# Layer norm statistics in two steps, the start of the reciprocal root on GpSimd, and one group of products with values

## What is computed

```python
def _layernorm(x, axis=-1, eps=1e-05):
    m = jnp.mean(x, axis=axis, keepdims=True)
    v = jnp.var(x, axis=axis, keepdims=True)
    return (x - m) / jnp.sqrt(v + eps)

def step(carry, blk):                      # one chunk of 128 tokens
    S, z = carry
    q_c, k_c, v_c = blk
    scores = jnp.einsum('bhcd,bhkd->bhck', q_c, k_c)
    scores = jnp.where(mask, scores, 0.0)
    num = jnp.einsum('bhck,bhke->bhce', scores, v_c) + jnp.einsum('bhcd,bhde->bhce', q_c, S)
    den = scores.sum(-1) + jnp.einsum('bhcd,bhd->bhc', q_c, z)
    S = S + jnp.einsum('bhkd,bhke->bhde', k_c, v_c)
    z = z + k_c.sum(axis=2)
    return ((S, z), (num, den))

xn = _layernorm(x, axis=-1)
x = x + attention(xn, w_attn, w_proj) + ffn(xn, gate_w, gate_b, expert_bias, w1, b1, w2, b2)
```

## Time and profile before

| what | value |
|---|---|
| median of 3 runs | 570.75 us (570.57 to 571.49) |
| the profiled execution | 570.87 us, its span 569.1 us |
| PE busy, whole span | 491.9 us, 86% |
| DVE busy | 430.7 us, 76% |
| ACT busy | 277.7 us, 49% |
| POOL busy | 283.8 us, 50% |
| first `scores` of the pipeline's steady part to its last | 38.11 to 289.65 us |

### The profile page before, as it was taken

How to read it: one execution, slowest core, us unless ns; L and a number is a source line. 1 busy time by engine, 2 the same in 40 slices (tenths; PEclk the granted TensorE clock), 3 DMA queues, 4 the chain that set the end, 5 groups by cost and what they waited for, 6 DMA issues and landing times.

```text
span 569.1 us, 17397 instructions
## 1 busy us (share of the span) xinstructions
PE 491.9 (86%) x6065; PEld 394.9 (69%) x6065; DVE 430.7 (76%) x917; ACT 277.7 (49%) x535; POOL 283.8 (50%) x448
## 2 busy tenths in 40 slices
PE   3599999899998999889985169989989989999992
PEld 1477877777877778677863068868868868877871
DVE  3779898998989899898776927766757666766671
ACT  0447767767777777667755023333333333333330
POOL 2645658666677576685553232343433443342421
PEclk9589999999999999999998569999999999999997
DMA  8322654645645546545323221212221222221000
GB/s 283 109 74 75 197 178 146 187 140 171 200 145 168 152 159 202 163 147 183 112 77 112 92 75 48 76 56 80 66 65 49 66 65 67 65 65 41 31 6 0
DMA packets 34016, 62.44 MB, mean 110 GB/s; under 512 B 5517, under 2 KB 9998, under 8 KB 33808
## 3 DMA queue, kind: packets, MB, share of 16 engines
q1 hardware_dynamic: 28944, 48.74, 27.5%
q0 software_dynamic: 4992, 12.60, 7.4%
HBM read 50.57 MB, written 13.50 MB: 113 GB/s over the span
## 4 chain that ended last, share of the span: by engine, by line
PE 73%; DVE 18%; issue 4%; DMA 1%; ACT 1%; POOL 1%; DVEq 0%; POOLq 0%; ACTq 0%
PE ps L551 19%; PE ps L565 18%; PE ps L380 6%; PE ps L342 5%; PE ps L407 4%; PE ps L391 3%; PE ps L448 3%; PE ps L421 3%; PE ps L434 3%; DVE rsn L604 2%; DVE AR L669 2%; PE ps L356 2%; PE ps L529 2%; DVE rsn L602 2%; PE ps L363 1%
## 5 line engine op out<-in xcount | busy, mean ns | idle before, releaser
L551 PEld LDWEIGHTS ps<-AR,W 128*128 x1872 | 131.6, 99 | 39.9 <-issue 1.0
L565 PE MATMUL ps<-W,ST 128*128 x624 | 150.8, 326 | 7.0 <-issue 7.0
L551 PE MATMUL ps<-AR,W 128*128 128x128 f16 x1872 | 155.8, 221 | 0.8 <-ACT AR L1038 0.8
L1097 POOL TENSOR_TENSOR W<-ST,W 128x512 f16<-128x512 f32 x64 | 74.4, 1162 | 79.9 <-ACT W L1001 79.7
L1137 POOL DMA_INDIRECT out<-AR x39 | 39.6, 1016 | 127.4 <-DVE AR L922 127.4
L890 DVE SCALAR_TENSOR_TENSOR ST<-ps,TAs,B1S 128x512 f32<-128x512 f32 x78 | 58.5, 749 | 58.7 <-PE ps L551 58.0
L1047 ACT ACTIVATE ST<-ST 128x512 f16<-128x512 f32 x78 | 49.2, 630 | 97.1 <-DVE ST L890 93.7
L669 DVE TENSOR_TENSOR AR<-ps,CT 128x512 f32<-128x512 f32 x128 | 82.0, 683 | 11.9 <-PE ps L380 11.9
L902 DVE SCALAR_TENSOR_TENSOR ST<-ST 128x512 f16<-128x512 f32 x78 | 53.6, 688 | 15.6 <-ACT ST L1047 15.2
L1132 POOL DMA_INDIRECT AR<-scr,AR x39 | 48.0, 1230 | 28.6 <-issue 11.0
L1088 POOL TENSOR_SCALAR AR<-AR,CT 128x256 f32<-128x256 f32 x64 | 59.3, 938 | 4.0 <-DVE AR L663 4.0
(11 more groups left out here) (145 smaller groups left out, 772.6 us busy)
## 6 DMA issues: line engine op xcount, KB each, us to landing
ST<-in_w SPq DMA_DIRECT2D x128, 256.0 KB, 4.2
scr<-XR SPq DMA_DIRECT2D x32, 256.0 KB, 2.1
XR<-in_x SPq DMA_DIRECT2D x32, 128.0 KB, 4.6
AR<-in_b SPq DMA_DIRECT2D x1, 1024.0 KB, 4.9
AR<-in_wall SPq DMA_DIRECT2D x1, 776.0 KB, 4.7
AR<-scr,AR POOLq DMA_INDIRECT x39, 3.6
out<-AR POOLq DMA_INDIRECT x39
AR<-in_wp SPq DMA_DIRECT2D x1, 256.0 KB, 5.1
```

The lines of the kernel that those rows point to most:

```text
L551: a = e.matmul(dst, W[:, off:off + 57472][:, bass.ds(at[s], 128)], XT16[s % 2][:, xl * 256 + k * 128:xl * 256 + (k + 1) * 128], start=(n = ...
L565: a = e.matmul(PS[4 + s % 2][:, 0:w], src[h % 4][:, fs], W[:, off:off + 57344 + w][:, bass.ds(at[s], w)], start=(f == 0 and w == 512), sto ...
L1097: e.tensor_tensor(lo_, src, hi, ALU.subtract).then_inc(p_wlo, 1)
```

## The change

`na` is split. `sums(c)` is the first instruction; `na(c)` is now the second alone, and stands on DVE behind `res` instead of ahead of it. Adding eps and the first guess go to GpSimd, to the head of `nn`: one instruction adds eps, one multiplies the variance's bits (as an integer) by -0.5 and adds the constant, so that three instructions on DVE become two on GpSimd. `nn` waits for the semaphore of `na` of the pair's second chunk.

The two halves of `pv` become one, at the end of TensorE's period. `inter` takes the place of the first half, begins the accumulation in PS[5] and waits for `y1` of the chunk before; only in a sequence's first chunk does `pv` begin it. Masks 0 and 1 now wait for the whole `pv` of the chunk before, not for its first half. On GpSimd `km` stands ahead of the first `w_lo`.

```diff
@@ tensor
             def inter(c):
...
+                e.wait_ge(S["y1"], c)
                 for g in range(2):
                     for i in range(2):
                         j = 2 * g + i
                         a = e.matmul(PS[5][:, j * 128:(j + 1) * 128], T32[:, g, 4 * i:4 * i + 4, :],
-                                     QK[c % 2][:, g * 128:(g + 1) * 128], start=False, stop=True,
+                                     QK[c % 2][:, g * 128:(g + 1) * 128], start=(j == 0), stop=True,
...
-            def pv(c, i):
-                e.wait_ge(s_[2 * i], c + 1)
-                e.wait_ge(s_[2 * i + 1], c + 1)
-                if i == 0:
-                    e.wait_ge(S["vh"], c + 1)
-                    if c >= 1:
-                        e.wait_ge(S["y1"], c)
...
+            def pv(c):
+                e.wait_ge(S["vh"], c + 1)
+                if c >= 1:
+                    e.wait_ge(S["y1"], c)
+                for i in range(2):
+                    e.wait_ge(s_[2 * i], c + 1)
+                    e.wait_ge(s_[2 * i + 1], c + 1)
...
+                                             start=(c % CPB == 0 and j == 0), stop=True, skip_group_check=True)
+                a.then_inc(S["pv"], 1)
...
                 if on(p - 3):
-                    pv(p - 3, 0)
+                    inter(p - 3)
                 mxa(p)
-                if on(p - 3):
-                    inter(p - 3)
...
                 if on(p - 3):
-                    pv(p - 3, 1)
+                    pv(p - 3)
@@ vector
+            def sums(c):
+                e.wait_ge(d_x[c % R], 16 * (c // R + 1))
+                if c >= 1:
+                    e.wait_ge(S["na"], c)
+                e.bn_stats(st6[:, :], XR[c % R][:, 256:512]).then_inc(S["sums"], 1)
+
             def na(c):
...
-                e.tensor_scalar(r_[:, 1], mv[:, c % 4 - 1:c % 4 + 1, 1], 1e-5, None, ALU.add).then_inc(dv.up(), 1)
-                e.wait_ge(dv.sem, dv.n)
-                e.tensor_scalar(r_[:, 2].bitcast(I32), r_[:, 1].bitcast(I32), 1, None,
-                                ALU.logical_shift_right).then_inc(dv.up(), 1)
-                e.wait_ge(dv.sem, dv.n)
-                e.tensor_scalar(r_[:, 0].bitcast(I32), r_[:, 2].bitcast(I32), -1.0, float(0x5f3759df),
-                                ALU.mult, ALU.add).then_inc(S["na"], 1)
+                e.bn_aggr(mv[:, c % 4, :], st6[:, :]).then_inc(S["na"], 1)
...
             def s_mask(c, r):
                 e.wait_ge(S["sc"], c + 1)
                 if c >= 1:
-                    e.wait_ge(pv_[r // 2], c)
+                    e.wait_ge(S["pv"], c)
...
                 if on(p + 2):
-                    na(p + 2)
+                    sums(p + 2)
                 if on(p - 4):
                     res(p - 4)
+                if on(p + 2):
+                    na(p + 2)
@@ gpsimd
             def nn(c):
...
-                e.wait_ge(S["na"], c // 2 + 1)
+                e.wait_ge(S["na"], c + 1)
+                if c >= 4:
+                    e.wait_ge(S["nb"], c - 3)
+                e.tensor_scalar(r_[:, 1], mv[:, c % 4 - 1:c % 4 + 1, 1], 1e-5, None, ALU.add).then_inc(po.up(), 1)
+                e.wait_ge(po.sem, po.n)
+                e.tensor_scalar(r_[:, 0].bitcast(I32), r_[:, 1].bitcast(I32), -0.5, float(0x5f3759df),
+                                ALU.mult, ALU.add).then_inc(po.up(), 1)
+                e.wait_ge(po.sem, po.n)
...
-                w_lo(2 * (p - 5))
                 if on(p - 2):
                     km(p - 2)
+                w_lo(2 * (p - 5))
```

More of the change, by code:

```diff
@@ L81, in program @@
         mv = sb("mv", [128, 4, 2], F32)
-        rsn = sb("rsn", [128, 2, 4, 2], F32)
+        rsn = sb("rsn", [128, 2, 2, 2], F32)
         nv = sb("nv", [128, 4], F32)
@@ L238, in program @@
         v_sq, t_sq, v_sv, a_wa, v_wa, v_bm = (sem(n) for n in ("v_sq", "t_sq", "v_sv", "a_wa", "v_wa", "v_bm"))
-        names = ("na", "nn", "nb", "xh", "xl", "xt", "xTc", "qk", "relu", "exp", "phi", "km", "sc", "ktr", "kt",
+        names = ("sums", "na", "nn", "nb", "xh", "xl", "xt", "xTc", "qk", "relu", "exp", "phi", "km", "sc", "pv", "ktr", "kt",
                  "vg", "vh", "lg", "in", "st", "t32", "y1", "yt1", "y", "yt2", "y2", "pr", "res")
@@ L244, in program @@
         s_ = [sem(f"s_s{i}") for i in range(4)]
-        pv_ = [sem(f"s_pv{i}") for i in range(2)]
         v_wmx, a_wsc, a_whi, p_wlo = (sem(n) for n in ("v_wmx", "a_wsc", "a_whi", "p_wlo"))
@@ L391, in inter @@
                         a = e.matmul(PS[5][:, j * 128:(j + 1) * 128], T32[:, g, 4 * i:4 * i + 4, :],
-                                     QK[c % 2][:, g * 128:(g + 1) * 128], start=False, stop=True,
+                                     QK[c % 2][:, g * 128:(g + 1) * 128], start=(j == 0), stop=True,
                                      skip_group_check=True)
                 a.then_inc(S["in"], 1)
-            def pv(c, i):
-                e.wait_ge(s_[2 * i], c + 1)
-                e.wait_ge(s_[2 * i + 1], c + 1)
-                if i == 0:
-                    e.wait_ge(S["vh"], c + 1)
-                    if c >= 1:
-                        e.wait_ge(S["y1"], c)
[L403 to L411, removed]
+            def pv(c):
[5 more added lines that the diff above has]
+                    e.wait_ge(s_[2 * i + 1], c + 1)
+                    for g in range(2):
+                        for t in range(2):
+                            for o in range(2):
+                                j, b = 2 * g + i, 2 * t + o
+                                a = e.matmul(PS[5][32 * b:32 * b + 32, j * 128:(j + 1) * 128],
+                                             V32[c % 2][:, 8 * g + 4 * i + b, :],
+                                             S32[2 * i + t][:, (2 * g + o) * 128:(2 * g + o + 1) * 128],
+                                             start=(c % CPB == 0 and j == 0), stop=True, skip_group_check=True)
+                a.then_inc(S["pv"], 1)
             def st(c):
@@ L588, in vector @@
             e.tensor_tensor(SQ, WF, WF, ALU.mult).then_inc(v_sq, 1)
-            def na(c):
-                xb, m, r_ = XR[c % R], mv[:, c % 4, :], rsn[:, c // 2 % 2, :, :]
-                e.wait_ge(d_x[c % R], 16 * (c // R + 1))
-                e.bn_stats(st6[:, :], xb[:, 256:512]).then_inc(dv.up(), 1)
-                e.wait_ge(dv.sem, dv.n)
-                e.bn_aggr(m, st6[:, :]).then_inc(dv.up(), 1)
-                e.wait_ge(dv.sem, dv.n)
-                if c % 2 == 0:
-                    return
+            def sums(c):
[3 more added lines that the diff above has]
+                e.bn_stats(st6[:, :], XR[c % R][:, 256:512]).then_inc(S["sums"], 1)
+            def na(c):
+                e.wait_ge(S["sums"], c + 1)
                 if c >= 4:
                     e.wait_ge(S["nn"], c // 2 - 1)
-                e.tensor_scalar(r_[:, 1], mv[:, c % 4 - 1:c % 4 + 1, 1], 1e-5, None, ALU.add).then_inc(dv.up(), 1)
-                e.wait_ge(dv.sem, dv.n)
-                e.tensor_scalar(r_[:, 2].bitcast(I32), r_[:, 1].bitcast(I32), 1, None,
-                                ALU.logical_shift_right).then_inc(dv.up(), 1)
-                e.wait_ge(dv.sem, dv.n)
-                e.tensor_scalar(r_[:, 0].bitcast(I32), r_[:, 2].bitcast(I32), -1.0, float(0x5f3759df),
-                                ALU.mult, ALU.add).then_inc(S["na"], 1)
+                e.bn_aggr(mv[:, c % 4, :], st6[:, :]).then_inc(S["na"], 1)
             def nb(c):
@@ L616, in nb @@
                                 ALU.subtract, ALU.mult).then_inc(S["nb"], 1)
+            sums(0)
             na(0)
+            sums(1)
             na(1)
@@ L976, in vh @@
                 if c >= 2:
-                    e.wait_ge(pv_[1], c - 1)
+                    e.wait_ge(S["pv"], c - 1)
                 e.activation(V32[c % 2][:, :, 0:16], PS[1][:, 0:256].rearrange("p (h e) -> p h e", h=16), ACT.Copy,
@@ L984, in y1 @@
             def y1(c):
-                e.wait_ge(pv_[1], c + 1)
+                e.wait_ge(S["pv"], c + 1)
                 if c >= 1:
@@ L1117, in gpsimd @@
                 w_lo(2 * (p - 5) + 1)
-            e.wait_ge(pv_[1], NC)
+            e.wait_ge(S["pv"], NC)
             for i in range(NG):
```

## The result

| | median | runs | span of the profiled execution |
|---|---|---|---|
| before | 570.81 us | 4 (570.57 to 571.49) | 569.1 us (570.87 us in all) |
| changed | 551.58 us | 4 (549.11 to 552.69) | 549.7 us (551.49 us in all) |

The ratio is 0.9655, 95% interval 0.9622 to 0.9689: 19.2 us less. The forecast was 551.2 us, range 544.0 to 558.0.

What follows compares the result with a forecast made beforehand. PE was taken to bound one period and `scores` waiting for `res` the next. From 570.87 us, 16.1 us for that wait and 3.6 us for one group of `pv` were subtracted, giving 551.2 us, range 544.0 to 558.0.

Steps and rivals of the forecast that it cites:

- What bounds the kernel: First stage: PE sets the pace in one period; in the next, `scores` waiting for `res` costs 1.1 us.
- The wait goes (16.1 us): DVE work ahead of `res` leaves, so all 13 waits of `scores` for `res`, 16.1 us in all, vanish.
- The price of L602 and L604 is GpSimd's: On DVE, these 2-element instructions (0.69 and 1.08 us) are held up until GpSimd's running instruction ends, not busy.
- What comes to GpSimd: Two new `nn` instructions at 0.28 us each; `nn` lasts 3.9 us, leaving 1.3 us before `nb`; no cost booked.
- The one group of `pv` (3.6 us): On PE, `yt2` starts earlier but 16 more passes precede `scores`; net 0.10 us per regular period, 3.6 us in all.
- The rival with 554.8 us: The one group of `pv` on PE is worth nothing, only the wait for `res` goes; chance 0.16.
- The sum: Whole kernel: 570.87 - 16.1 - 3.6 = 551.2 us, nothing booked at the first stage's ends.
- The signs: First stage: `scores` waits for `res` under 2 us, PE over 98% busy, `yt2` waits nearly every period, `nb` never for `nn`.
- L596 (now L600): Rival: on DVE behind `res`, this instruction is stretched by 0.9 us each period, giving 566.6 us; chance 0.08.
- The slower rival: On GpSimd, `nn` becomes the bound; with every link held up it lasts 10.8 us, giving 617 us; chance 0.02.
- The whole drain: Rival: on PE, each of 29 periods saves 0.37 us of tiling switches, 10.7 us, giving 544.1 us; chance 0.07.

Runs made afterwards that it cites:

- e1_stats_only: Kernel before with only the statistics part of the change; `pv` in two halves and `km` as before: 551.5 us against 568.68 us, ratio 0.9689.
- e3_km_first: Kernel before with only `km` moved ahead of the first `w_lo` on GpSimd: 564.15 us against 568.68 us, ratio 0.9897.
- e11_small_w_lo: Kernel before with GpSimd's `w_lo` cut to 2 elements from the fifth tile on, second stage using high halves; only first stage read: odd periods 8.01 us.
- e8_long_nn: Changed kernel with twelve more links in `nn` on GpSimd: 572.02 us against 570.13 us for the kernel before, ratio 1.0041.
- e5_late_yt2_one_group: Changed kernel with `yt2` behind `qk` and `pr` behind `vg` on TensorE: 546.7 us against 570.13 us for the kernel before, ratio 0.9588.

## Why the prediction was right, point by point

**What bounds the kernel.** PE in one period, `res` in the other: right. `e1_stats_only` removes the one and has the whole gain.

**The wait goes (16.1 us).** Right, and a little small: `e1_stats_only`, which has the statistics alone, gains 17.1 us over the 28 periods. Ten of the thirteen that waited lose 1.21 us each, where the timeline of before shows 1.14 of idle time, because the last group of `pv` overlaps the next one by 0.08 us only when there is no wait (0.65 us long, 0.57 to the next start). The three of a sequence's first chunk lose 1.64 us.

**The price of L602 and L604 is GpSimd's.** Right by `e3_km_first` and `e11_small_w_lo`. The Trainium skill (SBUF — State Buffer, "SBUF: two separate sides") says that for certain kinds of instruction the one of VectorE and GpSimd that starts first has the shared ports for its whole instruction, and the other blocks. Both runs agree: L602 took 1.16 us beside a `w_lo` of 1.16, and 0.20 beside one of 2 elements. The last section has a case that does not fit, beside `km`.

**What comes to GpSimd.** Two links at 0.31 and 0.27 us from start to start, 0.58 us for the pair, against my 0.56; the integer multiplication costs what the others cost (0.19 us). `nn` ended 3.75 us after `scores`, expected 3.8. The room behind it was 1.37 us in a regular period, expected 1.3. I had booked no cost, and there is none.

**The one group of `pv` (3.6 us).** This is the step that failed. Its mechanism was right to the hundredth: `yt2` at 3.71 us, waiting for `y`. Three sizes were off. Sixteen more passes cost 0.44 us, not 0.38, which was the weight loads' length and not the pitch of the group. After the wait PE takes 0.06 us more to `qk`. And in the periods with `mx`, `mxa` now stands between `inter` and `yt2`, so `yt2` starts at 3.93 us instead of 3.81, although `y` is there at 3.75. A regular period gained nothing instead of 0.10 us, one with `mx` 0.19 instead of 0.42, and a sequence's first chunk lost 0.44 instead of 0.38. In all that is nothing, where the sum had 3.6 us. The rival with 554.8 us, to which the prediction gave 0.16, had described this, as a case in which one of these terms slips.

**The sum** came out at 551.2 us although one term of it was empty, and that it met the measured 551.58 us so closely is luck. The steady stretch gave 17.05 us for the wait and the group together, where I had 19.7; the remaining 2.4 us of the profiled pair came at the ends, in part by the moment at which the clock rose, and the forecast had booked nothing there. The medians of the experiments put the change at 0.966 to 0.969, or 551 to 553 us from 570.8: between the forecast and that rival.

**The signs.** The waits of `scores` for `res` are gone, the masks start 1.21 us behind `scores`, and `yt2` waits for `y`, though not in the periods with `mx`. PE is busy over 98% in the regular periods and those with `mx`, but not in a sequence's last chunk, where it is 95% (7.57 of 7.96 us).

**The rivals.** L596 (now L600) was never held up, 0.183 us at most. The slower rival did not occur, and `e8_long_nn` shows its price. The whole drain could not be gained as the order stood; with `yt2` moved, `e5_late_yt2_one_group` has 0.32 of its 0.37 us in a regular period.

## What to carry to other kernels

The 2-element instructions that took four or six times their minimum here were not slow but held: look at what ends on the neighbouring engine at the same moment, and move either of the two. Before booking a gain on an engine that is busy all the time, look for the next input it will ask for sooner; here one group of matmuls saved 0.3 us a period only after the work that waited for `y` had been moved behind work that did not. A chain of small instructions off the critical engine is counted in links: here fourteen of 0.28 us fitted, and twenty-six came too late.

## What was not expected of the hardware

`nb` (L606), at 0.41 us in most periods, took 1.12 to 1.14 us in the periods with `mx` of the changed kernel, and there it ended 0.15 us after GpSimd's `w_lo`:

```profile
204.14 0.16 DVE L724 TENSOR_SCALAR SC<-ps 128x2 int32<-128x2 int32 x1
204.22 1.14 DVE L606 TENSOR_SCALAR AR<-XR,mv,rsn 128x256 f32<-128x256 f32 x1
```

```profile
204.05 1.16 POOL L1101 TENSOR_TENSOR W<-ST,W 128x512 f16<-128x512 f32 x1
```

L724, a TENSOR_SCALAR that reads PSUM (`ps`) and not SBUF, started just ahead of it beside the same `w_lo` and took its usual 0.16 us.

Beside `km`, which is a TENSOR_SCALAR on GpSimd, `nb` took 0.45 us in the kernel before, and 0.54 to 0.60 in the changed kernel (0.58 at 187.59 us, above). So `km` may cost it up to 0.2 us, but did not hold it for its own length, 0.9 us for each of its two instructions. Every hold-up to the end of GpSimd's instruction that was seen here, also those of L602 and L604, was by a TENSOR_TENSOR of GpSimd. Why the two kinds differ was not tried. The reductions and masks of DVE showed no hold-up in these stretches.
